# A stack of adapter products before a low-rank feed-forward block: A loaded in two requests with 1-KB runs, W transposed from 64-byte steps, another order of requests

## The reference, cut to what matters

```python
Bx  = einsum('bni,bri->bnr', x, B[ids])        # rank 16, B is cond_B (8 adapters)
c   = einsum('bnr,bor->bno', Bx, A[ids])       # A is cond_A, (8, 2048, 16)
base   = einsum('bsi,oi->bso', c, base_w) + base_b      # base_w is W, 2048 x 2048
hidden = einsum('bsi,ri->bsr', c, ffn_A)                # 64
logits = einsum('bsi,ei->bse', c, router_w)             # 16 experts
top-2 of softmax(logits), weights scaled to sum 1 -> combine (b, s, 16)
out = x + base + 0.5 * einsum('bse,bsr,eor->bso', combine, hidden, ffn_B)
```

## Time and profile before

| what | value |
|---|---|
| median of three executions | 471.47 us |
| the profiled execution | 471.14 us |
| its span (first to last instruction on the core) | 468.9 us |
| PE busy | 414.8 us, 88% |
| DVE busy | 298.5 us, 64% |
| ACT busy | 108.9 us, 23% |
| POOL busy | 48.2 us, 10% |
| moved by DMA | 135.31 MB, mean 289 GB/s |

### The profile page before, as it was taken

One profiled execution on the slowest core, in us unless ns is written; L12 is line 12 of the kernel. 1 busy time (PEld: TensorE's weight loads), 2 busy tenths in 40 slices (PEclk: granted clock), 3 DMA queues, 4 the chain that ended last, 5 costly groups with the idle time before them and its releaser, 6 DMA issues.

```text
span 468.9 us, 6167 instructions
## 1 busy us (share of the span) xinstructions
PE 414.8 (88%) x2240; PEld 278.2 (59%) x2240; DVE 298.5 (64%) x699; ACT 108.9 (23%) x166; POOL 48.2 (10%) x54
## 2 busy tenths in 40 slices
PE   0056879998988999999999999999999999999996
PEld 0045767777755566566556755655665566566675
DVE  1587249795636666757775677667567766767353
ACT  0011231425543432023002301310230132123210
POOL 3332000001200012002001200120120012002000
PEclk9999778999999999999999999999999999999999
DMA  8999999969997998899889989998997999655844
GB/s 201 202 359 343 353 358 365 297 189 355 296 302 154 271 342 303 290 291 370 293 282 328 335 273 293 369 323 270 293 363 264 293 336 325 241 192 180 300 170 180
DMA packets 97876, 135.31 MB, mean 289 GB/s; under 512 B 14068, under 2 KB 50932, under 8 KB 97844
## 3 DMA queue, kind: packets, MB, share of 16 engines
q1 hardware_dynamic: 67380, 102.07, 66.2%
q10 hardware_dynamic: 30466, 32.84, 24.0%
HBM read 99.24 MB, written 35.65 MB: 288 GB/s over the span
## 4 chain that ended last, share of the span: by engine, by line
PE 70%; DVE 11%; DMA 8%; ACTq 6%; issue 2%; ACT 1%; SPq 0%; DVEq 0%
PE ps L858 13%; PE ps L875 12%; PE ps L876 10%; PE ps L877 10%; PE ps L823 7%; PE ps L888 7%; PE ps L878 5%; DMA bexpT<-in_x 4%; DMA early_u<-in_L_ffn_B 4%; PE ps L813 4%; DVE h_r L673 4%; DVE xT L692 4%; ACTq L293 3%; DVE xbuf L801 2%; ACTq L278 2%
## 5 line engine op out<-in xcount | busy, mean ns | idle before, releaser
L801 DVE TENSOR_TENSOR xbuf<-ps,xbuf 128x512 f32<-128x512 f32 x128 | 86.9, 679 | 105.6 <-PE ps L878 105.3
L875 PE MATMUL ps<-h_r,u_r 128*128 128x512 f32 x256 | 109.3, 427 | 9.2 <-DVE xbuf L801 9.2
L876 PE MATMUL ps<-h_r,u_r 128*128 128x512 f32 x256 | 100.3, 392 | 0.0
L877 PE MATMUL ps<-h_r,u_r 128*128 128x512 f32 x256 | 100.1, 391 | 0.0
L823 PE MATMUL ps<-early 128*128 128x256 f32 x256 | 66.8, 412 | 33.2 <-DVE early L611 28.5
L875 PEld LDWEIGHTS ps<-h_r,u_r 128*128 128x128 f32 x256 | 48.0, 188 | 50.2 <-issue 20.1
L823 PEld LDWEIGHTS ps<-early 128*128 128x128 f32 x256 | 50.8, 207 | 45.4 <-issue 29.7
L692 DVE STREAM_TRANSPOSE xT<-xbuf 128x512 f32<-128x512 f32 x112 | 72.0, 681 | 0.0
L858 PE MATMUL ps<-bexpT,cur 128*32 128x512 f32 x512 | 61.6, 598 | 2.1 <-DVE h_r L673 2.1
L633 DVE STREAM_TRANSPOSE early<-xbuf 128x256 f32<-128x256 f32 x128 | 47.4, 415 | 19.5 <-PE ps L823 11.1
L464 ACT ACTIVATE h_r<-ps 128x512 fp32r<-128x512 f32 x64 | 35.7, 594 | 86.7 <-issue 54.3
(11 more groups left out here) (64 smaller groups left out, 228.5 us busy)
## 6 DMA issues: line engine op xcount, KB each, us to landing
out<-xbuf SPq DMA_DIRECT2D x31, 1024.0 KB, 7.1
xbuf<-in_x SPq DMA_DIRECT2D x30, 1024.0 KB, 7.0
xbuf<-in_x SPq DMA_DIRECT2D x28, 512.0 KB, 8.4
xbuf<-in_x ACTq DMA_DIRECT2D x28, 512.0 KB, 9.5
xbuf<-in_L_ffn_base_w SPq DMA_DIRECT2D x16, 512.0 KB, 13.5
xbuf<-in_L_ffn_base_w ACTq DMA_DIRECT2D x16, 512.0 KB, 12.7
gm_r<-g_hilo SPq DMA_DIRECT2D x128, 32.0 KB, 6.1
early_u<-in_L_ffn_B SPq DMA_DIRECT2D x14, 256.0 KB, 11.3
```

Source lines behind the costliest of these rows:

```text
L801: dve.tensor_tensor(xs, ps[:, ACC + t % 2, :], xs, ALU.add).then_inc(s_out, 1)
L875: pe.matmul(acc, u_r[:, b.q, 0, h, tok_t], hi, start=(h == 0), stop=False)
L876: pe.matmul(acc, u_r[:, b.q, 0, h, tok_t], lo, start=False, stop=False)
L877: pe.matmul(acc, u_r[:, b.q, 1, h, tok_t], hi, start=False, stop=False)
```

## The change

A's load becomes two requests, one of each queue, each for 64 partitions and all adapters; partition p holds the 16 neighbouring features 16p to 16p + 15, so every adapter gives a run of 1 KB. W's and ffn_A's views follow: part s takes the elements s, s + 16, s + 32, ... of a row's quarter, a step of 64 bytes. The tables of n and the written order of the requests are changed. POOL waits for the copies of A before it takes up the bias.

```diff
-    condA_q = cond_A.rearrange("n (q a l r) k -> n q l a (r k)", q=NQ, l=SQ, r=2)
+    condA_q = cond_A.rearrange("n (p r) k -> p n (r k)", p=P)
-        X_AT = {44 + 3 * j: j for j in range(KD)}
-        BX_AFTER = {66: 4, 92: 8}
-        SLOT_AT = {94: 8, 97: 9, 101: 10, 104: 11, 107: 12, 118: 13, 122: 14}
+        X_AT = {82 + 3 * j // 2: j for j in range(KD)}
+        BX_AFTER = {90: 4, 101: 8}
+        SLOT_AT = {103: 8, 106: 9, 109: 10, 112: 11, 115: 12, 119: 13, 123: 14}
...
-        E_AT = {20: 0, 26: 1, 34: 2, 40: 3, 52: 4, 60: 5, 70: 6, 78: 7, 95: 8, 102: 9, 109: 10, 117: 11}
-        E_LATE = {0: 12, 2: 13, 4: 14, 6: 15}
+        E_AT = {30: 0, 50: 1, 62: 2, 74: 3, 82: 4, 88: 5, 92: 6, 97: 7, 102: 8, 107: 9, 112: 10, 118: 11}
+        E_LATE = {1: 12, 2: 13, 5: 14, 6: 15}
-        E_FRESH, EIN_AT = 11, 94
-        PIECE_AT, X0_AT = {10: 4, 27: 5, 42: 6, 58: 7}, 26
+        E_FRESH, EIN_AT = 11, 103
+        PIECE_AT, X0_AT = {26: 5, 51: 6, 63: 7}, 31
...
-        def load_cond_a(eng, ns):
-            for n in ns:
-                for q in range(NQ):
-                    eng.dma_start(conda_q[q * SQ:(q + 1) * SQ, n, :, :], condA_q[n, q]).then_inc(s_conda, 16)
+        def load_cond_a(eng, h):
+            half = slice(h * (P // 2), (h + 1) * (P // 2))
+            eng.dma_start(conda_q[half], condA_q[half]).then_inc(s_conda, 16)
...
             load_w(sp, 3, (0, 1))
             load_experts(sp, 1, 0)
+            load_w(sp, 4, (0, 1))
             load_experts(sp, 2, 0)
-            load_w(sp, 4, (0, 1))
+            load_w(sp, 5, (0, 1))
             load_experts(sp, 3, 0)
+            load_x0(sp, (0, 1))
             load_experts(sp, 4, 0)
-            load_x0(sp, (0, 1))
-            load_w(sp, 5, (0, 1))
+            load_w(sp, 6, (0, 1))
+            store_g(0)
             load_experts(sp, 5, 0)
-            load_experts(sp, 6, 0)
-            store_g(0)
-            load_w(sp, 6, (0, 1))
-            load_experts(sp, 7, 0)
             load_w(sp, 7, (0, 1))
-            load_experts(sp, 8, 0)
+            store_g(1)
+            for g in range(6, 9):
+                load_experts(sp, g, 0)
+            sp.wait_ge(s_wt, 6 * KD)
+            for c in range(0, OC, 2):
+                load_xres(sp, 0, c)
             load_experts(sp, 9, 0)
-            store_g(1)
-            load_experts(sp, 10, 0)
             sp.wait_ge(s_gst, 32)
             for c in range(2):
                 load_gm(0, c)
-            sp.wait_ge(s_wt, 6 * KD)
-            for c in range(0, OC, 2):
-                load_xres(sp, 0, c)
+            load_experts(sp, 10, 0)
             load_experts(sp, 11, 0)
...
             ids = [adapter(pool, b) for b in range(NB)]
+            pool.wait_ge(s_a, NB)
             pool.wait_ge(s_bias, 32)
...
             act.dma_start(tok[:, :], itok.rearrange("(a b) -> a b", a=1)).then_inc(s_tok, 16)
             load_w(act, 0, (2, 3))
-            load_cond_a(act, range(NAD // 2, NAD))
+            load_cond_a(act, 1)
...
             load_experts(act, 1, 1)
+            load_w(act, 4, (2, 3))
             load_experts(act, 2, 1)
...
 def take_a():
-                dve.wait_ge(s_conda, 16 * NAD * NQ)
+                dve.wait_ge(s_conda, 32)
                 for b in range(NB):
-                    dve.tensor_copy(a_t[:, :, b * RK:(b + 1) * RK].rearrange("p (a r) k -> p a r k", r=2),
-                                    conda_q[:, bass.ds(ids[b], 1), :, :]
-                                    .rearrange("p n a (r k) -> p (n a) r k", r=2)).then_inc(s_a, 1)
+                    dve.tensor_copy(a_t[:, :, b * RK:(b + 1) * RK],
+                                    conda_q[:, bass.ds(ids[b], 1), :].rearrange("p n (r k) -> p (n r) k", k=RK))\
+                       .then_inc(s_a, 1)
 def ffna_transposes():
-                by_r = ffna_q.rearrange("p t (a l r) -> p r a t l", l=SQ, r=2)
-                to_r = ffnaT.rearrange("p (a r) (t l) -> p r a t l", r=2, l=SQ)
-                for r in range(2):
-                    dve.transpose(to_r[:, r], by_r[:, r]).then_inc(s_fat, 1)
+                by_r = ffna_q.rearrange("p t (l r) -> p r t l", l=SQ)
+                to_r = ffnaT.rearrange("p r (t l) -> p r t l", l=SQ)
+                for h in range(2):
+                    part = slice(h * KD // 2, (h + 1) * KD // 2)
+                    dve.transpose(to_r[:, part], by_r[:, part]).then_inc(s_fat, 1)
 def w_transpose(n):
-                src = w_in[g % WB].rearrange("p t (a l r) -> p a r t l", l=SQ, r=2)[:, s // 2, s % 2]
+                src = w_in[g % WB].rearrange("p t (l r) -> p r t l", l=SQ)[:, s]
```

More of the change, by code:

```diff
@@ L139, in carve @@
             return flat[:, at:at + n]
-        conda_q = carve(0, D).rearrange("p (n a f) -> p n a f", n=NAD, f=2 * RK)
+        conda_q = carve(0, D).rearrange("p (n f) -> p n f", n=NAD)
         condb_q = carve(D, D).rearrange("p (t d) -> p t d", t=P // SQ)
@@ L318, in _ @@
             load_w(sp, 0, (0, 1))
-            load_cond_a(sp, range(0, NAD // 2))
+            load_cond_a(sp, 0)
             for row in (64, 96):
```

## The result

The changed kernel took 485.1 us (median of four executions, 483.77 to 487.79) against 471.93 for the kernel before: a ratio of 1.0276, interval 1.022 to 1.0333. It is slower, outside the range of 448 to 480, and 27 us from the forecast. The profiled execution is the slowest of the four (487.79, span 485.6).

The account below looks back on a forecast made before the run. It took DVE's work up to the last W transpose as the bound: 84 + 134x, 111.5 us instead of 126.8. Giving back 2 us for transfers leaves 13.3 off 471.14, 457.8, so a median of 458 us; range 448 to 480.

Parts of the forecast that it names:

- The sum: DVE's work and waits up to the last W transpose: 84 + 134x, 111.5 us, 15.3 before 126.8.
- the paragraph on the order of requests: Queues before the last W transpose: x0 lands at 65.5 instead of 68.9, DVE waits 1.3 us, x0 and W6 not late.
- W at 64-byte steps: DVE's W transposes: 64-byte steps cost 0.205 us more each, 26 us for 128; ffn_A's two add 1.2.
- Forecast x: Extra time of one W transpose on DVE at 64-byte steps, taken from a reduction's row at 0.8 ns an element.
- The dear steps: Rival: W transposes set the pace of the whole stretch, no first-batch gain, 478 us (472 to 484); chance 0.26.
- A's loads: Opening transfers: W0 lands at 9.2 instead of 12.35, A at 12.2 instead of 19.1, later pieces about 8 us sooner.
- The copies and the bias: DVE's eight copies of A take 2.2 us instead of 9.1; POOL's later bias work costs nothing.
- The third rival: Before the last W transpose, half clock prevails or x0 and W6 come late: 12 us back, 469 us; chance 0.10.
- Its sign: The third rival holds if PE shows half clock over more than 15 us before the last W transpose.

Follow-up runs that it names:

- f2: Changed kernel with the first g store and W6 ahead of expert 4 on SP, W6 ahead of expert 1's copy on ACT: 482.21 us, 1.0198.
- f3: Changed kernel with ACT's x0 requests behind its first g copy, and the first g store and W6 requested sooner: 473.37 us, 1.0021.
- a3: Changed kernel's two-request A load and held bias, with the tables, request order and 8-byte steps of the kernel before: 468.94 us, 0.9929.
- a2: Changed kernel's two-request A load, 64-byte steps and held bias, with tables and request order of the kernel before: 476.61 us, 1.0108.
- b1: Kernel before with only POOL's bias work held until A is copied: 472.08 us, 1.0014.
- g3: Changed kernel with both queue stalls mended, A in two requests, and 8-byte steps (features unpaired): 470.13 us, 0.9959.

## Why the prediction was wrong

**The step that failed is "The sum", with the paragraph on the order of requests under it.** It added up DVE's work and allowed 9.3 us of waits (5 + 1.3 + 3). The rows had shown that DVE waited much more than that: 126.8 us less 12.35 and 76.9 us of work, some 37 us. I let these waits go, although of them I had named and removed only the 4.35 us for A and most of the 6.64 for x0 (the 7 us saved in the copies of A are work, not a wait). In the changed kernel DVE begins at 11.67 us, works 89.6 us and waits 39.3 up to 140.6; the sum had 9.2, 93.0 and 9.3, which make 111.5. The start is 2.5 us late and the work 3.4 us less than forecast; the term that failed is the waits, by 30 us. Two of them alone are 20.6 us. The sum took DVE's work for the bound, and DVE was not the bound.

Inside it, two sentences were false. "SP stands ... before expert 4 until flip 1 (n = 50, about 47), with x0, W6 behind: neither is late": the flip's date came from DVE's pace, and PE flipped at 70.96 us, so that behind it W6 stood some 7 us and the g store, not even named, some 22 (f2 issues them at 66.03 and 52.40). And what stands behind ACT's x0 requests was not asked. The row that I had read has two requests in 0.82 us; in the changed kernel these two took 3.27 and 5.16, with the copy of g behind them. The trace of the kernel before had the warning, in ACT's order of time:

```profile
42.49 4.11 ACTq L272 DMA_DIRECT2D bexpT<-in_x  x1
```

f3, which mends these two places alone, gives back 11.7 us.

**W at 64-byte steps: right in kind, a little large.** Forecast x = 0.205 us, found 0.16 to 0.17 (0.50 less 0.335); the median duration is 0.572 us, just below the 0.58 to 0.65 named. The reduction's row gave 0.73 to 0.98 ns an element; the transposes show about 0.65. At 128 of them that is 21 us of work, of which 6.6 to 8.2 reach the last W transpose and 3 to 8 the time: neither all, as the sum had it, nor none. The dear steps did not happen. Their time, 478 (472 to 484), is the nearest of all to the 485.1 measured, but by luck: the loss has another cause.

**A's loads: right in sign, half in size.** W0 was taken up at 11.67, forecast 9.2 (12.35 before). By then the transfers had moved 2.8 MB, of which W0 is 2.1: it did not have the engines to itself. A landed at 16.2, forecast 12.2, and PE began at 18.18, forecast 15. "About 8 us sooner" for all later pieces shrank to 3 or 4 at x0, as seen in a3 and a2 (66.11 and 64.69 instead of 69.00). In the changed kernel DVE came to x0 at 94.52 us, forecast about 64.

**The copies and the bias: right, and in the old order worth nothing.** Eight copies at 0.29 us, POOL's bias from 17.99 on beside transposes at their usual pace (14 in 7.11 us). But b1 shows the 7 us absorbed: in the old order x0's landing is the next date, and it did not move.

**The third rival** (clock and new order eat it) came nearest in its cause, late transfers in the new order, but with 12 us where 27 were lost. Its sign, more than 15 us of half clock, could not decide anything: read from windows of 4 us, the changed kernel has some 31 us of it up to the last W transpose, but the kernel before already had some 17. From about 46 to 62 us the half clock stands without a break; it came while PE waited 11.97 us for DVE, up to 52.98. What it costs beside the stalls was not measured apart.

## What to carry to other kernels

Sum up an engine's work only where it is the bound; elsewhere list each wait of the trace, and say of each what now ends it. When requests are reordered, write for every queue what stands behind each waiting request, and date the wait from the engine that releases it. A request issued while the transfers are full can hold the engine that issues it (here for up to 5.16 us), so nothing urgent of ScalarE's belongs behind it; and time saved ahead of a transfer that lands no sooner is worth nothing (b1).

## What the runs showed of the hardware

A DVE transpose of 128x256 float32 takes 0.39 to 0.45 us from adjacent elements or 8-byte steps and 0.55 to 0.67 from 16, 32 or 64 bytes. Copies of 128x256 on DVE, 0.28 us each, took up to 4.58 us while POOL worked on one partition, and 0.28 or 0.29 once POOL was held; transposes beside the same POOL work kept their pace. The two requests of 1 MB for x0 took ACT 3.27 and 5.16 us to issue in the changed kernel, while the transfers were full (DMA share 1.07); the two of 512 KB for W1 took SP 0.82 us together. No kernel that computes the reference came out faster than the one before; the two that ran faster (a3, g3) did so with unpaired features.
